# Gated cross block on one core: weight sums and low parts all on VectorE, the second norm's 1/std started on ScalarE, and the front's steps in other places

## What is computed

```python
x = x + tanh(g_xattn[0]) * wkv(time_decay, time_first, layernorm(x), ctx)     # scan over 256 tokens
n = layernorm(x)                                                               # over 512 channels
hidden = fwht(silu(n @ W1.T) * (n @ W3.T))                                     # 512 -> 2048
x = x + tanh(g_ffn[0]) * (hidden @ W2.T)                                       # 2048 -> 512
```

## Time and profile before

| | us |
|---|---|
| median of 3 runs | 1139.82 (1139.08 to 1140.48) |
| the profiled execution's own time | 1142.86 |
| its span, first to last instruction | 1141.0 |
| PE busy | 1023.8 (90%) |
| DVE busy | 858.4 (75%) |
| ACT busy | 396.8 (35%) |
| POOL busy | 375.0 (33%) |

### The profile page before, as it was taken

How to read it: one execution, slowest core, us unless ns; L and a number is a source line. 1 busy time by engine, 2 the same in 40 slices (tenths; PEclk the granted TensorE clock), 3 DMA queues, 4 the chain that set the end, 5 groups by cost and what they waited for, 6 DMA issues and landing times.

```text
span 1141.0 us, 18280 instructions
## 1 busy us (share of the span) xinstructions
PE 1023.8 (90%) x6892; PEld 688.7 (60%) x6892; DVE 858.4 (75%) x1315; ACT 396.8 (35%) x685; POOL 375.0 (33%) x278
## 2 busy tenths in 40 slices
PE   5698968667798999999899899999899999999998
PEld 2364423245576776666667576667667666677775
DVE  7847997868778886898778786888778986664334
ACT  6755331131422541233423341234422442232221
POOL 0133868645742115221341115221341114211111
PEclk9998998878899999999999999999999999999999
DMA  9967427346464445264354445264454442344341
GB/s 344 342 232 286 173 98 283 129 148 221 148 240 161 147 169 207 85 231 184 119 215 167 150 159 210 75 240 171 135 213 167 170 163 90 132 148 184 148 148 38
DMA packets 40909, 201.74 MB, mean 177 GB/s; under 512 B 8944, under 2 KB 18288, under 8 KB 29808
## 3 DMA queue, kind: packets, MB, share of 16 engines
q1 hardware_dynamic: 40816, 200.52, 47.9%
HBM read 171.12 MB, written 29.38 MB: 176 GB/s over the span
## 4 chain that ended last, share of the span: by engine, by line
issue 34%; PE 26%; DVE 10%; POOL 8%; DMA 2%; ACT 1%; POOLq 0%; DVEq 0%; SPq 0%; ACTq 0%
PE pl L721 3%; PE pl L723 3%; PE pl L722 3%; POOL work L1633 3%; PE po L733 3%; PE po L735 3%; PE pg L721 3%; PE pg L723 3%; PE pg L722 3%; POOL bv L1556 2%; PE po L744 1%; PE po L742 1%; DVE work L1400 1%; DMA factor_rows<-tiny 1%; DVE x L1331 1%
## 5 line engine op out<-in xcount | busy, mean ns | idle before, releaser
L1633 POOL TENSOR_TENSOR work<-work 128x512 bf16<-128x512 f32 x112 | 146.4, 1309 | 567.3 <-DVE work L1482 567.3
L733 PE MATMUL po<-work,w 128*128 128x512 f16 x456 | 173.3, 380 | 1.7 <-DVE x L1331 0.7
L735 PE MATMUL po<-work,w 128*128 128x512 f16 x456 | 172.9, 379 | 0.0
L1024 ACT ACTIVATE work<-work 128x256 f32<-128x256 f32 x168 | 68.1, 415 | 271.8 <-DVE work L1400 271.6
L721 PE MATMUL pg<-wts 128*128 128x256 f16 x448 | 124.0, 277 | 24.1 <-DVE work L1400 24.1
L721 PE MATMUL pl<-xn,wts 128*128 128x256 f16 x448 | 123.9, 277 | 0.0
L723 PE MATMUL pg<-wts 128*128 128x256 f16 x448 | 123.9, 277 | 0.0
L722 PE MATMUL pg<-wts 128*128 128x256 bf16 x448 | 123.9, 277 | 0.0
L721 PE MATMUL pl<-wts 128*128 128x256 f16 x448 | 123.9, 276 | 0.0
L722 PE MATMUL pl<-xn,wts 128*128 128x256 bf16 x448 | 123.8, 276 | 0.0
L723 PE MATMUL pl<-xn,wts 128*128 128x256 f16 x448 | 123.7, 276 | 0.0
(11 more groups left out here) (196 smaller groups left out, 2296.4 us busy)
## 6 DMA issues: line engine op xcount, KB each, us to landing
wts<-up_stage SPq DMA_DIRECT2D x56, 2048.0 KB, 8.1
up_stage<-wts SPq DMA_DIRECT2D x8, 1024.0 KB, 7.4
up_stage<-wts SPq DMA_DIRECT2D x16, 512.0 KB, 3.3
ev<-ctx_t SPq DMA_DIRECT2D x7, 1024.0 KB, 5.7
xin<-x_t SPq DMA_DIRECT2D x7, 1024.0 KB, 4.9
bv<-x_tok SPq DMA_DIRECT2D x7, 1024.0 KB, 7.1
out_t<-x SPq DMA_DIRECT2D x7, 1024.0 KB, 4.4
wts<-w_t SPq DMA_DIRECT2D x11, 512.0 KB, 6.4
```

Of the source, the lines that this page charges most:

```text
L733: pe.matmul(po[:, d, :], w2h[:, j, d * P:d * P + P], hh[:, b, :], start=start, stop=False, skip_group_check=True)
L735: pe.matmul(po[:, d, :], w2l[:, j, d * P:d * P + P], hh[:, b, :], start=False, stop=False, skip_group_check=True)
L1024: act.activation(sg[:, slot, cols], src, ACT.Silu).then_inc(acted, 1)
L1633: pool.tensor_tensor(hl[:, b, :], hf[:, slot, :], hh[:, b, :], ALU.subtract).then_inc(pair_lo, 1)
```

## The change

1. `weight_sums` moves from POOL to DVE, with the low part. Four differences become three operations (the first does two blocks at once). It stands at other places: units 0 to 6 in the first chunk, 7 to 15 in run 2, each **ahead of** the four joins of its pair. SP's puts and second loads follow.
2. The low parts of the hidden values move from POOL to DVE (`low`), right after the two high parts.
3. 1/std of the second norm: DVE adds eps (`var_plus_eps`); ACT does Ln and then Exp with scale -0.5 (`rstd_guess` at the end of pair 5, `rstd_begin` in pair 6 between the two kinds of copies); DVE does one Newton step (`refine`).
4. Steps of the front: `logs` at the end of pair 1; the numerator's tokens all in pair 2; both corrections at the head of pair 3; residuals of the two batches in pairs 3 and 4; `tok_moments_of` from pair 5 to pair 6, between `var_plus_eps` and `refine`; PE's variance product (`var_full`) in pair 5 behind the last products.
5. In the first chunk, weight units 13 to 15 are converted later (slots 9 to 11), and the last two use other places.

```diff
-SUMS_AT = {3: 0, 4: 1, 5: 2, 6: 3, 7: 4, 9: 5, 11: 6, 13: 7, 14: 8, 15: 9}
-LATE_SUMS = {0: (10, 11), 1: (12, 13), 2: (14, 15)}
-LATE_LO = {0: (9, 10), 1: (11, 12), 2: (13, 14), 3: (15,)}
+SUMS_AT = {3: (0,), 5: (1,), 9: (2,), 10: (3, 4), 11: (5,), 13: (6,)}
+LATE_SUMS = {0: (7,), 1: (8,), 2: (9,), 3: (10, 11), 4: (12, 13), 5: (14, 15)}
...
-                if front and p == 5:
-                    var_full(front_of(run))
                 for w in range(2):
                     pe.wait_ge(joined, g * 6 + (3 + w))
                     part(run, p, 3, w, fifth[w], False, True)
                     part(run, p, 4, w, chain[w], False, True).then_inc(product[4][w], 1)
+                if front and p == 5:
+                    var_full(front_of(run))
...
+            def rstd_guess(run):
+                act.wait_ge(newton, run.nth_full(0, X1_STEPS))
+                act.activation(rstd, var_eps, ACT.Ln).then_inc(rstd_log, 1)
+
+            def rstd_begin(run):
+                act.wait_ge(rstd_log, run.nth_full(0, 1))
+                act.activation(rstd, rstd, ACT.Exp, scale=-0.5).then_inc(rstd_first, 1)
...
                     keep_first(run, p)
+                    if front and p == 6:
+                        rstd_begin(ahead)
                     keep_sixth(run, p)
...
                     if front and p == 2:
-                        logs(ahead)
                         inverses(ahead)
...
                     pair_silu(run, p, 5, 0, 1)
+                    if front and p == 1:
+                        logs(ahead)
+                    if front and p == 5:
+                        rstd_guess(ahead)
...
+            def refine(run):
+
+                dve.wait_ge(rstd_first, run.nth_full(0, 1))
+                dve.tensor_tensor(newton_tmp, rstd, rstd, ALU.mult).then_inc(newton, 1)
...
+            def weight_sums(n):
+
+                b = unit_blocks(n)
+                dve.wait_ge(traw_loaded[n % TRAWS], 16 * (n // TRAWS + 1))
+
+                dve.tensor_tensor(b[:, 0:2, :].rearrange("p k (s n) -> p s k n", s=2),
+                                  b[:, :, P:].rearrange("p (s k) n -> p s k n", s=2),
+                                  b[:, 0:2, :].rearrange("p k (s n) -> p s k n", s=2), ALU.subtract).then_inc(wsum, 1)
+                dve.wait_ge(wsum, 3 * n + 1)
+                dve.tensor_tensor(b[:, 2:4, P:], b[:, 2:4, P:], b[:, 0:2, 0:P], ALU.subtract).then_inc(wsum, 1)
+                dve.wait_ge(wsum, 3 * n + 2)
+                dve.tensor_tensor(b[:, 2:4, 0:P], b[:, 2:4, 0:P], b[:, 2:4, P:], ALU.subtract).then_inc(wsum, 1)
...
                 dve.tensor_scalar(tout[n % 2][:, 0:KT * PW], traw[n % TRAWS], F16_MAX, -F16_MAX, ALU.min,
                                   ALU.max).then_inc(wsum_hi, 1)
+                dve.wait_ge(wsum_hi, n + 1)
+                dve.tensor_tensor(tout[n % 2][:, KT * PW:].bitcast(BF16), traw[n % TRAWS], tout[n % 2][:, 0:KT * PW],
+                                  ALU.subtract).then_inc(wsum_lo, 1)
...
                     if front and p == 5:
                         centre(ahead)
+                    if front and p == 6:
+                        var_plus_eps(ahead)
                         if more:
                             tok_moments_of(front_of(ahead))
-                    if front and p == 6:
-                        rsqrt(ahead)
+                        refine(ahead)
...
+                    if run.is_front(2):
+                        for n in LATE_SUMS.get(p, ()):
+                            weight_sums(n)
...
                     high(p, 0, g * 3 + 3)
+                    low(p, 1, g * 2 + 1)
+                    low(p, 0, g * 2 + 2)
+
+            def low(p, slot, made):
+                b = 2 * (p % 2) + slot
+                dve.wait_ge(pair_hi, made)
+                dve.tensor_tensor(hl[:, b, :], hf[:, slot, :], hh[:, b, :], ALU.subtract).then_inc(pair_lo, 1)
...
+            def pairs(run):
                 ahead = front_of(run)
...
+                quotient(ahead)
+                channel_sum(ahead, 0)
+                channel_sum(ahead, 1)
```

More of the change, by code:

```diff
@@ L531, in _ @@
             load_again(4)
-            put_plain(6)
+            load_v(2)
             put_sums(2)
             load_again(5)
[L535 to L540, removed]
             load_x(2)
             load_tokens(2)
+            put_plain(6)
+            for n in range(3, 5):
+                put_sums(n)
+                load_again(n + TRAWS)
+            put_plain(7)
             put_sums(5)
@@ L545, in _ @@
             load_pair(Run(2), 0)
+            spread_factors(Run(3))
             put_sums(6)
             load_again(9)
[L548 to L550 removed]
             load_pair(Run(2), 1)
@@ L1248, in residual @@
                     dve.wait_ge(gains, 2)
-                for i, b in enumerate(run.batches):
-                    dve.wait_ge(y_done, run.before + (i + 1))
-                    dve.scalar_tensor_tensor(out=batch_cols(x1[:, run.par, :, :], b), in0=batch_rows(bv, b),
-                                             scalar=gt[:, 0:1], in1=batch_cols(xin, b), op0=ALU.mult,
-                                             op1=ALU.add).then_inc(x1_done, 1)
+                dve.wait_ge(y_done, run.before + (1 if run.half else b + 1))
+                dve.scalar_tensor_tensor(out=batch_cols(x1[:, run.par, :, :], b), in0=batch_rows(bv, b),
+                                         scalar=gt[:, 0:1], in1=batch_cols(xin, b), op0=ALU.mult,
+                                         op1=ALU.add).then_inc(x1_done, 1)
             def turned_lo(b):
@@ L1441, in pairs @@
                     join(run, p, 7, 1, early1[:, 1, T:], 1, 1)
-                    if run.is_front(2) and p in (0, 1, 2, 3):
-                        for n in {0: (9, 10), 1: (11, 12), 2: (13, 14), 3: (15,)}[p]:
-                            wsum_hi_of(n)
                     if front and p == 0:
@@ L1603, in ffn @@
                         tile_clamp(15)
-                    if j in SUMS_AT:
-                        weight_sums(SUMS_AT[j])
                     hidden_lo(run, j)
-                    if j - 1 in SUMS_AT:
-                        weight_sums_lo(SUMS_AT[j - 1])
-            def pairs(run, front=True):
+            def pairs(run):
                 ahead = front_of(run)
-                for p in range(PAIRS):
-                    g = run.pair(p)
-                    if run.is_front(2):
-                        for n in LATE_SUMS.get(p, ()):
-                            weight_sums_lo(n - 1)
-                            weight_sums(n)
-                    if front and p == 3:
-                        quotient(ahead)
-                    if run.is_front(2) and p == 3:
-                        weight_sums_lo(15)
-                    if front and p == 4:
-                        channel_sum(ahead, 0)
-                    if front and p == 5:
-                        channel_sum(ahead, 1)
-                    for slot in (1, 0):
-                        b = 2 * (p % 2) + slot
-                        if run.is_front(2) and p == 0:
-                            pool.wait_ge(down, Run(1).down(SLOTS - LAG - 1))
-                        else:
-                            pool.wait_ge(pair_down, g * KT)
-                        pool.wait_ge(pair_hi, g * 2 + (2 - slot))
-                        pool.tensor_tensor(hl[:, b, :], hf[:, slot, :], hh[:, b, :],
-                                           ALU.subtract).then_inc(pair_lo, 1)
+                quotient(ahead)
+                channel_sum(ahead, 0)
+                channel_sum(ahead, 1)
             pool.memset(ones[:, :], 1.0 / D).then_inc(ones_set, 1)
@@ L1657, in _ @@
             pairs(Run(7, 0, 3))
-            pairs(Run(8, 1, 3), front=False)
 def kernel(x, ctx_2048, g_xattn, g_ffn, L0_xattn_time_decay, L0_xattn_time_first,
```

92 lines of the change are left out of this document (46 added, 46 removed).

## The result

Slower, as forecast: 1171.97 us in the median of 4 runs (1171.91 to 1176.02), against 1139.45 for the kernel before on the same chip (4 runs, 1134.94 to 1140.48). The ratio is 1.0302, with a 95% interval of 1.0267 to 1.0337. The forecast was 1168 us, range 1150 to 1184. The profiled execution took 1171.91 us with a span of 1170.1.

The account below looks back on a forecast made before the run. Neither PE nor DVE was full in a loop run, some 12 us being waits; DVE and POOL together paced first chunk and run 2. First chunk -11, run 2 +11, runs 3 to 6 +34, run 7 -6: +28, 1168 us, range 1150 to 1184.

Parts of the forecast that it names:

- The stall of pair 7: Start of pair 7, runs 2 to 6: PE waits for late weights, +14.6 us a run including 2.1 of slow clock.
- Rival (a): Start of pair 7: its load comes in time, so the kernel gets faster, 1093 us; chance 4%.
- Rival (b): Stall stays, but unloading POOL gives more in first chunk, and run 2 is no longer than before: 1143 us; 7%.
- Rival (d): Moving low parts and sums does nothing, first chunk 0, rest as forecast: 1179 us; no chance of its own.
- Pairs 0 to 5: First six pairs of a loop run: shorter waits from the moved front steps, -6.1 us a run.
- Low parts: Every pair of a run: low parts on DVE cost +1.3 us a pair, mostly given back, +0.3 us a run.
- rival (c): VectorE becomes the bound, high parts stay at 1.15 us, heads late in pairs 1, 3 and 6: 1190 us; 5%.
- Run 2: Run 2 as a whole, with weight sums on DVE and the stall: 162 against 151 us, +11 us.
- A unit on DVE: ... 3.5 us: Run 2's pair heads: one weight-sum unit on DVE costs 3.5 us, worked out by operation size.
- 4 of slow clock: Run 2, counted beside pairs 0 to 5: 4 us for the lower clock level.
- First chunk: 104 to 230 us: less POOL work lets the chunk end at 219 against 229.9, -11 us.
- DVE gains 7 x 3.5 and loses 11 high parts of 0.7 and the 5.3: +12: First chunk: DVE's own work rises by 12 us while POOL loses about 65 of its 92.

Follow-up runs that it names:

- Experiment 1: The change with SP issuing pair 7's weight load ahead of spread_factors instead of behind it: 1092.53 us, 0.9594.
- 3: The kernel before with only the first norm's statistics moved from pair 5 to pair 6: 1207.08 us, 1.0578.
- 4: The kernel before with only SP's order altered, pair 7's load ahead of spread_factors: 1137.09 us, 0.9979.
- experiment 8: The change with the factors stored as they lie, 8 values of a partition side by side in DRAM: 1119.10 us, 0.9833.
- experiment 5: Experiment 1 with the low parts of the hidden values back on GpSimd: 1087.56 us, 0.9549.
- 12: The kernel before with only the second norm's 1/std begun by ScalarE (Ln, Exp, one Newton step): 1131.91 us, 0.9942.
- experiment 6: Experiment 1 with the weight sums, their places and SP's order for them as in the kernel before: 1099.20 us, 0.9662.
- 9: Experiment 5 with the second weight-sum unit of pairs 3, 4 and 5 of run 2 behind the joins: 1074.61 us, 0.9448.
- 11: Experiment 5 with the factors read back later, behind the load of the next run's pair 0: 1087.11 us, 0.9559.
- experiment 7: Experiment 1 with 1/std made by VectorE alone again, guess and nine Newton operations: 1127.31 us, 0.9909.
- experiment 2: The change with the first norm's statistics moved back from pair 6 to pair 5, SP's order unchanged: 1118.04 us, 0.9799.

## Why the prediction was right, and where it was not

**The stall of pair 7**, +14.6 us a run: right in place, cause and size, and more than the whole result. Pairs 6 and 7 of runs 3 to 6 took 13.9 to 15.8 us more than before, 14.6 in the mean. In run 4 the statistics were ready 7.2 us into pair 6 (7.4), store 10.96 (11.6), load 9.05 (8.1 to 9.1), pair 7 at 27.9 (28.1), then, over the five runs, a pair of 15.9 to 17.7 (16.5). Experiment 1 removes it by SP's order alone, 3 makes it by the statistics' place alone, and 4 shows that it wasn't there before. The slow clock behind the stall, 2.1 us, was right too; the columns are those of the earlier trace rows:

```profile
636.00:640.00 4.00, 4.00 (x24) 2.92 (x22) 0.00 (x0) 0.59 (x1) 0.00 (x0) 0.57 0.71 299
```

Most of these 4 us are at the lower level of 1.2 GHz, as the 4.4 us behind a gap in the kernel before were. Rival (a), the load in time, is what experiment 1 builds: 1092.5 against the 1093 that I gave it. Its condition, a faster store, is what experiment 8 shows in part. Rival (b) had run 2 no longer than before; it took 19.2 more. Rival (d) had the first chunk unchanged; it ended 17.7 earlier.

**Pairs 0 to 5**, -6.1 us a run: -6.5 in run 4 (the first six distances, 89.96 against 96.49). Pair 1 +0.5, pair 2 -1.0, pair 3 -3.6, pair 5 -2.3. The four runs of the loop together +32.3 for +34, run 7 -5.2 for -6.

**Low parts**, +0.3 us a run: right, some 0.5 between experiments 5 and 1; rival (c), VectorE as the bound, falls with experiment 5 (not 10 us faster) and with the high parts at 0.43 throughout. The Trainium skill (Perfetto Trace Analysis, "Optimizing Scalar/DVE Operations") says that moving work between these two might not help, as they share an SBUF port; the trace agrees, with 0.5 us a run the worse for it.

**Run 2**, +11: wrong, +19.2. Two terms of pairs 0 to 5 failed. The first is the weight units' price: "A unit on DVE: ... 3.5 us". One alone took 3.58. But I costed all nine as if POOL were quiet, though my own terms kept POOL's channel sums in pairs 4 and 5, where two units each stand. DVE and POOL of the change in pair 4:

```profile
293.96 2.46 DVE L1378 TENSOR_TENSOR wts<-wts 128x256 f32<-128x256 f32 x1
296.45 1.37 DVE L1380 TENSOR_TENSOR wts<-wts 128x256 f32<-128x256 f32 x1
...
300.52 0.42 DVE L1378 TENSOR_TENSOR wts<-wts 128x256 f32<-128x256 f32 x1
```

```profile
293.41 2.73 POOL L1594 TENSOR_TENSOR psum<-x 128x1024 f32<-128x1024 f32 x1 [26.26 <-DVE x L1266]
296.22 1.32 POOL L1603 TENSOR_TENSOR psum<-psum 128x512 f32<-128x512 f32 x1
```

3.83 us for two operations that take 0.84 alone: +3.0 in pair 4, and 3.48 instead of 0.84, +2.6, in pair 5 likewise. What PE felt of it are its waits for the joins of pairs 4 and 5, where I had the heads over by 1.7 and 2.9:

```profile
304.51 0.28 PE L720 MATMUL pg<-wts 128*128 128x256 f16 x1 [3.71 <-DVE work L1443]
...
325.99 0.39 PE L720 MATMUL pg<-wts 128*128 128x256 f16 x1 [5.29 <-DVE work L1443]
```

That is 4.4 us more. In pair 3 PE's gaps were 7.2 for 6.2, 1.6 of them for products of DVE that the quotient held up, where I had allowed 0.9. The second term is "4 of slow clock". In pairs 0 to 5 the clock was at the lower level for 20.5 us (2 x 3.4, 6.8 and 2 x 3.4), PE was busy for 17.7 of them, and half of that, 8.9 us, is what it cost: 4.9 more. With 1.3 more in pair 6 these are more than the 8.2 us by which I was off, since pair 0 was 0.6 shorter than I had it and pair 1 waited 2.7 us for its joins and not 4.2.

**First chunk**, -11: wrong, -17.7. The step that failed is "DVE gains 7 x 3.5 and loses 11 high parts of 0.7 and the 5.3: +12". DVE's busy time did not rise by 12 us, it fell by 9.2, from 109.4 to 100.2. The term leaves out what POOL's sums had cost all the other operations of DVE there, though I had counted just that for the low parts in the loop. Two kinds of them, before and after (xcount, busy us, mean ns):

```profile
L1337 DVE TENSOR_SCALAR wts<-wts 128x1024 f16<-128x1024 f16 x6 | 5.3, 891 | 0.0
L1191 DVE TENSOR_TENSOR ev<-ev 128x1028 f32<-128x1028 f32 x2 | 4.8, 2425 | 0.0
```

```profile
L1364 DVE TENSOR_SCALAR wts<-wts 128x1024 f16<-128x1024 f16 x6 | 2.5, 419 | 0.0
L1206 DVE TENSOR_TENSOR ev<-ev 128x1028 f32<-128x1028 f32 x2 | 2.4, 1226 | 0.0
```

The kinds of operation that occur equally often in both traces between 104 us and run 2 took 21 us less together, which is the difference between +12 and -9. In experiments 12 and 6, with the sums on POOL, the like comparison gives 0.9 and 0.5 us more.

How the gain splits can't be read from where run 2 begins, because the start of the kernel scatters by several us from trace to trace: the slot that begins at 99.45 in the kernel before begins at 93.9 in experiment 6 and 97.1 in 12, which are the same program up to there, and at 93.7 to 98.8 in experiments 5, 9 and 11, which are the same program up to run 2. Counted from that slot to the start of run 2, the kernel before takes 130.5 us (130.5 and 130.6 in experiments 4 and 3), experiments 12 and 6 take 126.2, experiment 7 121.1, and the change 114.5, as the others with both parts do to within 3 (114.5 to 117.4). So 1/std is worth 4.3 and the sums' move, with the later conversions, 8.8 to 11.7, and the two about add. Of the 17.7 us, 1.7 lie ahead of that slot and are scatter.

The sum of +28 for a measured +29.1 is thus better than its parts, and that is luck: the first chunk was 6.7 us better than I had it and run 2 was 8.2 worse. Both go back to an oversight of one kind, that what POOL does beside an operation of DVE belongs to its price.

## What to carry to other kernels

A step that is moved takes with it whatever its result feeds, and in an in-order DMA queue everything behind the wait for it: 5 us of work moved one pair later cost 14 us a run, and one call placed behind a load gave 79 back. Before counting what an engine saves, list what each queue holds behind the moved result, and place the issue of a wait that can be late after the loads that can't. Price an operation by a row from the place where it will stand, since the same one cost 0.42 or 2.46 us, and count what work that goes gives back to all that stays beside it (21 us in the first chunk). Put filler work where its engine waits for another (12 us here) and not ahead of what that engine owes.

## What the runs showed of the hardware

- A store of 1024 single fp32 values takes 11.0 to 11.6 us, and 1.4 us in rows of 8 values: some 10 ns for each value that stands alone. I had expected the latter to be longer.
- VectorE and GpSimd seem to take turns rather than to share: an operation of 0.16 us lasted 2.01 us, as long as the GpSimd operation that began 0.02 us before it (experiment 2).
- ScalarE loads a table for the logarithm and another for the exponential, 1.28 us each, though the first can be done ahead: in the change, ahead of the wait for its input.

```profile
605.09 1.28 ACT L909 ACT_TABLE_LOAD   x1
609.61 0.63 ACT L909 ACTIVATE wide<-wide 128x512 f32<-128x512 f32 x1 [3.24 <-DVE wide L1290]
...
611.22 1.28 ACT L913 ACT_TABLE_LOAD   x1
```
